# Window attention in eight chunks: scores of four images at once, and gelu as one image and then three

## The chip, the cores and the metric

One core of a Trainium2 chip. The metric is the device time of one launch in microseconds (us). Engines are named as in the profile: PE (TensorE) with PEld, its weight loads; DVE (VectorE); ACT (ScalarE); POOL (GpSimd); SP (SyncE).

## The reference

The kernel computes one block of a windowed transformer on x of shape 4 x 32 x 64 x 64 (images, channels, height, width), all in fp32. A window is 8 x 8 pixels, so 64 tokens of 32 channels; there are 4 heads of 8 channels. In short:

```python
xw = windows_of(x)                                  # (-1, 64, 32)
h = _ln(xw, ln1_g, ln1_b)
q, k, v = split(h @ qkv_w.T + qkv_b)                # 4 heads
attn = softmax(einsum('whnd,whmd->whnm', q * hd ** (-0.5), k) + bias)
o = einsum('whnm,whmd->whnd', attn, v)
xw = xw + (o @ proj_w.T + proj_b)
h = _ln(xw, ln2_g, ln2_b)
h = gelu(h @ fc1_w.T + fc1_b)                       # 32 -> 128
xw = xw + (h @ fc2_w.T + fc2_b)                     # 128 -> 32
```

## The kernel before

The four images lie on the 128 partitions, 32 channels each. The work is cut into NCH = 8 chunks; a chunk is one row of 8 windows in each image, 512 tokens. One chunk's attention has 8 units: a unit is four windows of one image, a tile of 128 x 512 scores.

PSUM has eight banks of 128 x 512. Before, S_PS is banks 0 and 1 (scores), T_PS banks 2 and 3 (transposed scores), FA and FB banks 4 and 5 (front: centering, variance, k, q, v), O_PS and D_PS banks 6 and 7 (attention output, projection, second norm).

Every engine runs its own program in order, counting semaphores tie the programs together, and the order is written out by hand. All but the closing loop is one software pipeline over c. In iteration c the *front* works for chunk f = c + 1, the scores for c, and the *back* for p = c - 1. The path of a unit is:

- `score` (PE, L656): q against masked keys, K = 32 rows of one image at row group C * g, windows in the two column halves. One call makes two units (two images) in the two S_PS banks and waits until both were read (`biased`).
- `add_bias` (DVE, L472) reads the bank, adds the table and writes one of six buffers s_sb; `find_max` (DVE, L482) takes the row maxima; `subtract_max` (POOL, L207) subtracts them. POOL also does `mask_keys` (L198) and `norm2` (L214).
- `turn` (PE, L677) transposes two units into the two T_PS banks; `exp_round` (ACT, L250) takes the exponential of both in one instruction.
- `attend` (PE, L691) multiplies four units by v and sums them for the denominator; `inv_den` (ACT, L311) and `divide` (DVE, L499) finish the softmax. t = 0 and 1 are the halves of a chunk.

The front of a chunk is `center1` (L620), `square1` (ACT, L258), `variance1` (L623), `inv_std1` (ACT, L264: Ln, then Exp), `norm1` (DVE, L490), `make_k` (L637), `make_v` (L648), `make_q` (L645), and ACT's `copy_k` (L272: a plain copy, two masked), `copy_v` (L296) and `copy_q` (L289). The back is `project` (L719), `residual` (DVE, L510), `center2` (L725), `keep2` (DVE, L515), `square2` (ACT, L320), `variance2` (L732), `inv_std2` (ACT, L326), `norm2`. Products of 64 x 64 tiles come from two helpers, `straight` (L605) and `crossed` (L611), which fill different tiles of the array, so one call of each stands side by side: variance2 with center1, make_k with project, make_q with center2. These three are called pairs. The PE order of an iteration is at L785 to L834: four scores, r = 0 to 3, with other work between each.

`up` (PE, L735) makes the hidden layer of a chunk, one image to a bank: banks 0 to 3 for chunk 0 and the odd ones (`low`), banks 3 to 6 for the rest, so bank 3 is shared. `gelu` (ACT, L334) takes two images to an instruction, those with the shared bank first; `down` (PE, L755) and `add_y` (DVE, L560) finish, and SP stores. up(0), gelu(0) and down(0) run in the last iterations; the closing loop (L836 to L841) does chunks 1 to 7. `up(c)` waits for the first gelu of chunk c - 1 alone (L744).

## Time and profile before

| What | us |
|---|---|
| Runs shown | 188.22, 189.28, 192.5 (median 189.28) |
| Profiled execution, its time | 188.29 |
| Profiled execution, its span | 186.6 |
| PE busy | 169.2 (91%) |
| ACT busy | 129.2 (69%) |
| DVE busy | 120.2 (64%) |
| PEld busy | 92.4 (50%) |
| POOL busy | 91.4 (49%) |

Busy is the union of an engine's instructions. Several matmuls can run at a time in different tiles of the array, so PE's busy time is less than the sum of its records. An fp32 matmul of the program gives two records.

### The profile page before, as it was taken

Reading aid. Unit: us, or ns where it says so; the run is one execution under the profiler, and the core shown is the slowest. Engines: PE = TensorE matmul, PEld = TensorE weight load, DVE = VectorE, ACT = ScalarE, POOL = GpSimd, SP = SyncE. Lnnn points to the kernel's source line nnn. Section 1 sums busy time; section 2 is a strip of 40 time slices with the busy share of each in tenths; the row PEclk is TensorE's granted clock in tenths of the full one; section 3 lists DMA queues with packets and bytes.
Section 4 is the critical chain, followed back from the end, with each engine's and each line's share of the span. In section 5 each row is a group of like instructions: output and inputs, shape, how many; then the busy total and the mean of one; then the engine's idle time right before and its main releaser. Section 6 shows DMA issues by size and latency. Waiting matters only on the chain.

```text
span 186.6 us, 6349 instructions
## 1 busy us (share of the span) xinstructions
PE 169.2 (91%) x2688; PEld 92.4 (50%) x2688; DVE 120.2 (64%) x220; ACT 129.2 (69%) x180; POOL 91.4 (49%) x103
## 2 busy tenths in 40 slices
PE   7976999999999999999999999999999878738882
PEld 7642465566456546565565565455655533102210
DVE  3486965978687677869786977677697821403222
ACT  4546595569677866868696779677843385798881
POOL 7402674647492856567484937584766540020000
PEclk9999999999999999999999999999999999999999
DMA  2840000000000000000000000000000000001323
GB/s 71 231 174 4 0 2 4 4 4 2 4 4 0 4 4 2 4 5 0 4 4 4 0 4 5 0 4 0 4 5 4 0 4 0 29 27 56 116 112 112
DMA packets 3245, 4.71 MB, mean 25 GB/s; under 512 B 946, under 2 KB 1298, under 8 KB 3218
## 3 DMA queue, kind: packets, MB, share of 16 engines
q1 hardware_dynamic: 2840, 4.23, 6.7%
q8 instruction: 21, 0.34, 0.8%
q0 software_dynamic: 256, 0.07, 0.4%
q14 instruction: 6, 0.05, 0.1%
q10 hardware_dynamic: 122, 0.01, 0.0%
HBM read 2.21 MB, written 2.10 MB: 23 GB/s over the span
## 4 chain that ended last, share of the span: by engine, by line
PE 67%; DVE 10%; ACT 10%; issue 5%; DMA 3%; POOL 3%; ACTq 1%; DVEq 0%; POOLq 0%
PE ps L670 17%; PE ps L686 12%; PE ps L605 9%; PE ps L704 9%; PE ps L711 7%; DVE s_sb L477 7%; ACT hid L342 5%; PE ps L651 4%; PE ps L751 4%; PE ps L629 3%; DMA raw_b<-in_L_conv_rpb_dram 3%; POOL raw_b L193 2%; DVE mx L487 1%; ACT rstd L330 1%; ACT pt L255 1%
## 5 line engine op out<-in xcount | busy, mean ns | idle before, releaser
L211 POOL TENSOR_TENSOR s_sb<-s_sb,mx 128x512 f32<-128x512 f32 x64 | 66.6, 1045 | 61.1 <-DVE mx L487 61.1
L477 DVE TENSOR_TENSOR s_sb<-ps,bias_t 128x512 f32<-128x512 f32 x64 | 43.9, 686 | 26.0 <-PE ps L670 25.0
L487 DVE TENSOR_REDUCE mx<-s_sb 128x8 f32<-128x512 f32 x64 | 43.9, 686 | 2.2
L670 PE MATMUL ps<-k_m,q_sb 32*64 32x256 f32 x512 | 35.0, 387 | 2.9 <-DVE s_sb L477 2.1
L686 PEld LDWEIGHTS ps<-ident,s_sb 128*128 128x128 f32 x256 | 27.5, 140 | 17.7 <-issue 10.3
L255 ACT ACTIVATE pt<-ps 128x1024 f32<-128x1024 f32 x32 | 32.5, 1016 | 5.1 <-PE ps L686 4.2
L686 PE MATMUL ps<-ident,s_sb 128*128 128x128 f32 x256 | 34.9, 279 | 0.0
L670 PEld LDWEIGHTS ps<-k_m,q_sb 32*64 32x64 f32 x512 | 16.4, 131 | 15.2 <-DVE s_sb L477 5.6
L704 PEld LDWEIGHTS ps<-pt,v_blk 128*32 128x32 f32 x1024 | 15.0, 110 | 8.1 <-ACT pt L255 6.0
L704 PE MATMUL ps<-pt,v_blk 128*32 128x64 f32 x1024 | 17.6, 220 | 1.5 <-ACT pt L255 1.5
L342 ACT ACTIVATE hid<-ps,fb 128x1024 f32<-128x1024 f32 x16 | 17.0, 1110 | 2.0 <-PE ps L751 2.0
L605 PE MATMUL ps<-h,wqk 64*64 64x512 f32 x64 | 17.0, 613 | 1.2 <-DVE h L494 1.2
L611 PE MATMUL ps<-x_sb,cent_m 64*64 64x512 f32 x64 | 17.2, 614 | 0.9 <-DVE x_sb L512 0.9
L562 DVE SCALAR_TENSOR_TENSOR y_sb<-ps,vec,x_sb 128x512 f32<-128x512 f32 (+1 forms) x9 | 6.2, 691 | 17.2 <-PE ps L765 17.2
L711 PE MATMUL ps<-pt,ones_h 128*32 128x256 f32 x256 | 16.7, 379 | 0.0
L217 POOL TENSOR_TENSOR h_sb<-h_sb,rstd 128x512 f32<-128x512 f32 x8 | 10.3, 1282 | 12.4 <-ACT rstd L332 12.4
L316 ACT ACTIVATE den<-ps 128x256 f32<-128x256 f32 x16 | 6.1, 384 | 11.0 <-PE ps L711 11.0
L506 DVE TENSOR_TENSOR att<-ps,den 128x256 f32<-128x256 f32 x16 | 6.7, 420 | 10.2 <-ACT den L318 10.2
L751 PE MATMUL ps<-h_sb,f_s 32*128 32x512 f32 x64 | 9.1, 637 | 4.5 <-ACT hid L342 4.5
L262 ACT ACTIVATE sq<-ps 128x512 f32<-128x512 f32 x8 | 4.8, 598 | 10.1 <-PE ps L611 10.1
L280 ACT ACTIVATE k_sb<-ps,bq 128x512 f32<-128x512 f32 x8 | 5.5, 688 | 9.0 <-PE ps L605 7.8
L651 PEld LDWEIGHTS ps<-wv,h 128*64 128x64 f32 x256 | 8.1, 138 | 6.5 <-issue 6.5
(92 smaller groups left out, 190.5 us busy)
## 6 DMA issues: line engine op xcount, KB each, us to landing
x_sb<-in_x_dram SPq DMA_DIRECT2D x8, 256.0 KB, 4.8
out_dram<-y_sb SPq DMA_DIRECT2D x7, 256.0 KB, 2.0
out_dram<-y_sb SPq DMA_DIRECT2D x2, 128.0 KB, 1.8
raw_b<-in_L_conv_rpb_dram POOLq DMA_DIRECT2D x8, 8.0 KB, 2.7
f_nat<-in_L_conv_fc_w_dram SPq DMA_DIRECT2D x2, 16.0 KB
w_nat<-in_L_conv_qkv_w_dram ACTq DMA_DIRECT2D x1, 12.0 KB
p_nat<-in_L_conv_proj_w_dram SPq DMA_DIRECT2D x1, 4.0 KB
vec_r<-in_L_conv_ln_g_dram ACTq DMA_DIRECT2D x1, 0.1 KB
```

The costliest lines, as they stand in the source:

```text
L211: pool.tensor_tensor(tile, tile, mx[:, n % 4, :].unsqueeze(2).to_broadcast([128, 2 * NH, NT]), ALU.subtract).then_inc(shifted, 1)
L255: act.activation(pt[:, n % 8:n % 8 + 2, :, :, :].rearrange("p u a k n -> p (u a k n)"), ps[:, 2:4, :].rearrange("p u n -> p (u n)"), ACT.E ...
L342: act.activation(hid[:, c % 2, 2 * pair:2 * pair + 2, :].rearrange("p g n -> p (g n)"), ps[:, b:b + 2, :].rearrange("p g n -> p (g n)"), A ...
L477: dve.tensor_tensor(s_sb[:, n % NSB, :, :, :].rearrange("p a h m -> p a (h m)"), S_PS[u].rearrange("p (a k) -> p a k", a=2), bias_t[:, :, ...
L487: dve.reduce_max(mx[:, n % 4, :], s_sb[:, n % NSB, :, :, :].rearrange("p a h m -> p (a h) m"), AX.X)\
L605: ins = pe.matmul(out[r:r + 64, :], w[r:r + 64, r:r + 64], rhs[r:r + 64, :], start=True, stop=True, tile_position=(r, r))
L611: ins = pe.matmul(out[64 - r:128 - r, :], w[r:r + 64, r:r + 64], rhs[r:r + 64, :], start=True, stop=True, tile_position=(r, 64 - r))
L670: ins = pe.matmul(S_PS[u][NT * ab:NT * (ab + 1), 256 * pr:256 * (pr + 1)], q_sb[C * g:C * (g + 1), c % 2, NT * w:NT * (w + 1)], k_m[C * g: ...
L686: ins = pe.transpose(T_PS[u][:, 128 * i:128 * (i + 1)], s_sb[:, n % NSB, pr, 2 * hp:2 * hp + 2, :].rearrange("p h m -> p (h m)"), ident[:, :])
L704: ins = pe.matmul(OD_PS[t][C * g:C * (g + 1), NT * wl:NT * (wl + 1)], v_blk[:, c % 2, G * (4 * t + wl) + g, 32 * (1 - hp):32 * (2 - hp)], ...
L711: ins = pe.matmul(OD_PS[t][C * g:C * (g + 1), 256:512], ones_h[:, hp, :], pt[:, (4 * t + g) % 8, :, hp, :], start=(hp == 0), stop=(hp == 1 ...
L751: ins = pe.matmul(ps[:, first_bank(c) + g, :], f1_s[C * g:C * (g + 1), :], h2_sb[C * g:C * (g + 1), c, :], start=True, stop=True, tile_pos ...
```

## The change

A score now makes four units, all four images, in four banks: `score(c, t)`, t = 0, 1. There are 2 calls of 32 records to a chunk, where there were 4 of 16; the transposes, exponentials, DVE and POOL instructions stay as many. The banks are dealt anew: 0 to 3 scores, bank 0 also variance1, make_v and make_q, bank 1 also attend(c, 0); 4 and 5 transposed scores; 6 (X_PS) center1 and make_k; 7 (Y_PS) attend(p, 1), project, center2, variance2.

The order of PE in iteration c becomes: score(c, 0), pair variance2(p-1)/center1(f), turn(p, 3), variance1(f), attend(p, 1), turn(c, 0), score(c, 1), turn(c, 1), pair make_k(f)/project(p), make_v(f), attend(c, 0), pair make_q(f)/center2(p), turn(c, 2). The other engines follow it: inv_den and divide of the first half move from the next iteration to this one, the Exp of inv_std2 moves behind an exponential, copy_v comes straight behind copy_k, copy_q behind inv_den. make_q now waits for copy_v, which reads its bank, and so does the very first score. up(0) moves ahead of attend(7, 1). In `gelu` the first instruction takes the one image in the shared bank, the second the three others. Not shown below: the same names in add_bias, find_max, subtract_max, the copies and the set-up, where only bank or index names change.

```diff
-        S_PS = [ps[:, 0, :], ps[:, 1, :]]
-        T_PS = [ps[:, 2, :], ps[:, 3, :]]
-        FA, FB = ps[:, 4, :], ps[:, 5, :]
-        O_PS, D_PS = ps[:, 6, :], ps[:, 7, :]
-        OD_PS = [O_PS, D_PS]
+        S_PS = [ps[:, g, :] for g in range(G)]
+        T_PS = [ps[:, 4, :], ps[:, 5, :]]
+        X_PS, Y_PS = ps[:, 6, :], ps[:, 7, :]
+        OD_PS = [S_PS[1], Y_PS]
...
             for c in range(-1, NCH + 2):
                 f = c + 1
-                for r in range(3):
-                    if there(c):
-                        subtract_max(c, r, 0)
-                        subtract_max(c, r, 1)
-                    if r == 0 and there(c - 2):
-                        norm2(c - 2)
+                if there(c):
+                    for g in range(G):
+                        subtract_max(c, 0, g)
+                if there(c - 2):
+                    norm2(c - 2)
+                if there(c):
+                    subtract_max(c, 1, 0)
                 if f >= 1 and there(f):
                     mask_keys(f)
                 if there(c):
-                    subtract_max(c, 3, 0)
-                    subtract_max(c, 3, 1)
+                    for g in range(1, G):
+                        subtract_max(c, 1, g)
...
+            def log_var2(p):
                 act.wait_ge(var2_ready, p + 1)
                 if p >= 1:
                     act.wait_ge(h2_ready, p)
-                act.activation(rstd2[:, :], FB, ACT.Ln, bias=eps[:, :]).then_inc(log2, 1)
+                act.activation(rstd2[:, :], Y_PS, ACT.Ln, bias=eps[:, :]).then_inc(log2, 1)
+
+            def inv_std2(p):
                 act.wait_ge(log2, p + 1)
                 act.activation(rstd2[:, :], rstd2[:, :], ACT.Exp, scale=-0.5).then_inc(rstd2_ready, 1)
...
-                for pair in ((1, 0) if low(c) else (0, 1)):
-                    b = first_bank(c) + 2 * pair
-                    act.activation(hid[:, c % 2, 2 * pair:2 * pair + 2, :].rearrange("p g n -> p (g n)"),
-                                   ps[:, b:b + 2, :].rearrange("p g n -> p (g n)"),
+                shared = 3 - first_bank(c)
+                for images in (slice(shared, shared + 1), slice(0, 3) if low(c) else slice(1, 4)):
+                    banks = slice(first_bank(c) + images.start, first_bank(c) + images.stop)
+                    act.activation(hid[:, c % 2, images, :].rearrange("p g n -> p (g n)"),
+                                   ps[:, banks, :].rearrange("p g n -> p (g n)"),
                                    ACT.Gelu, bias=fb1[:, :]).then_inc(gelu_ready, 1)
 
             for c in range(-1, NCH + 2):
                 f, p = c + 1, c - 1
-                if there(p):
-                    inv_den(p, 0)
                 if there(f):
                     square1(f)
                 if c == 0:
                     blank_values(1)
                 if there(p - 1):
+                    log_var2(p - 1)
+                if there(p):
+                    exp_round(p, 3)
+                if there(f):
+                    inv_std1(f)
+                if there(p - 1):
                     inv_std2(p - 1)
                 if there(p):
-                    exp_round(p, 3)
-                if there(f):
-                    inv_std1(f)
-                if there(p):
                     inv_den(p, 1)
-                if there(c):
-                    exp_round(c, 0)
-                if there(f):
-                    copy_k(f)
-                    if f == 0:
-                        copy_q(f)
-                    if f == 0:
-                        copy_v(f)
-                if there(c):
-                    exp_round(c, 1)
-                if f >= 1 and there(f):
-                    copy_v(f)
-                if f >= 1 and there(f):
-                    copy_q(f)
                 if p == NCH - 1:
                     act.preload_act_table_set("gelu_and_others")
                     gelu(0)
                     act.preload_act_table_set("natural_log_exp_and_others")
+                if there(c):
+                    exp_round(c, 0)
+                    exp_round(c, 1)
+                if there(f):
+                    copy_k(f)
+                    if f == 0:
+                        copy_q(f)
+                    copy_v(f)
+                if there(c):
+                    inv_den(c, 0)
+                if f >= 1 and there(f):
+                    copy_q(f)
                 if there(p):
                     square2(p)
...
             for c in range(-1, NCH + 1):
                 f, p = c + 1, c - 1
                 if there(c):
-                    add_bias(c, 0, 0)
-                    find_max(c, 0, 0)
-                    add_bias(c, 0, 1)
-                    find_max(c, 0, 1)
-                if there(p):
-                    divide(p, 0)
-                if there(c):
-                    add_bias(c, 1, 0)
-                    find_max(c, 1, 0)
-                    add_bias(c, 1, 1)
-                    find_max(c, 1, 1)
+                    for g in range(G):
+                        add_bias(c, 0, g)
+                        find_max(c, 0, g)
                 if there(f):
                     norm1(f)
                 if there(p):
                     divide(p, 1)
                 if there(c):
-                    add_bias(c, 2, 0)
-                    find_max(c, 2, 0)
+                    for g in range(2):
+                        add_bias(c, 1, g)
+                        find_max(c, 1, g)
                 if there(p):
                     residual(p)
                 if there(c):
-                    add_bias(c, 2, 1)
-                    find_max(c, 2, 1)
-                    add_bias(c, 3, 0)
-                    find_max(c, 3, 0)
+                    for g in range(2, G):
+                        add_bias(c, 1, g)
+                        find_max(c, 1, g)
+                    divide(c, 0)
                 if there(p):
                     keep2(p)
-                if there(c):
-                    add_bias(c, 3, 1)
-                    find_max(c, 3, 1)
...
             def wait_center1(f):
                 pe.wait_ge(x_in[f], 16)
                 if f >= 1:
-                    pe.wait_ge(v_copied, f)
+                    pe.wait_ge(k_copied, f)
+                if f >= 2:
+                    pe.wait_ge(k_scaled, f - 1)
...
             def variance1(f):
                 pe.wait_ge(squared1, f + 1)
-                if f >= 3:
-                    pe.wait_ge(log2, f - 2)
                 if f >= 1:
-                    pe.wait_ge(q_copied, f)
-                pe.matmul(FB, mean_m[:, :], sq1[:, :], start=True, stop=True).then_inc(var1_ready, 1)
+                    pe.wait_ge(biased, unit_of(f - 1, 0, 0) + 1)
+                pe.matmul(S_PS[0], mean_m[:, :], sq1[:, :], start=True, stop=True).then_inc(var1_ready, 1)
 
...
             def wait_q(f):
-                pe.wait_ge(k_copied, f + 1)
                 if f >= 1:
-                    pe.wait_ge(k_scaled, f)
+                    pe.wait_ge(v_copied, f + 1)
...
             def make_v(f):
+                if f >= 1:
+                    pe.wait_ge(biased, unit_of(f - 1, 1, 0) + 1)
+                else:
+                    pe.wait_ge(log1, 1)
                 for w in range(NW):
                     for hh in range(2):
-                        ins = pe.matmul(FA[NT * hh:NT * (hh + 1), NT * w:NT * (w + 1)], h1[:, f % 2, w, :],
+                        ins = pe.matmul(S_PS[0][NT * hh:NT * (hh + 1), NT * w:NT * (w + 1)], h1[:, f % 2, w, :],
                                         wv[:, hh, :, :].rearrange("p k d -> p (k d)"), start=True, stop=True,
                                         tile_position=(0, NT * hh))
...
-            def score(c, r):
-                if r == 0:
+            def score(c, t):
+                if t == 0:
                     pe.wait_ge(q_copied, c + 1)
                     pe.wait_ge(k_masked, c + 1)
                     if c >= 1:
                         pe.wait_ge(k_scaled, c)
-                n = unit(c, r, 0)
-                if n >= 2:
+                        pe.wait_ge(divided, 2 * (c - 1) + 1)
+                    else:
+                        pe.wait_ge(v_copied, 1)
+                elif there(c + 1):
+                    pe.wait_ge(log1, c + 2)
+                n = unit_of(c, t, 0)
+                if n:
                     pe.wait_ge(biased, n)
                 for pr in range(2):
                     for ab in range(2):
-                        w = 4 * (r // 2) + 2 * pr + ab
-                        for u in range(2):
-                            g = 2 * (r % 2) + u
-                            ins = pe.matmul(S_PS[u][NT * ab:NT * (ab + 1), 256 * pr:256 * (pr + 1)],
+                        w = 4 * t + 2 * pr + ab
+                        for g in range(G):
+                            ins = pe.matmul(S_PS[g][NT * ab:NT * (ab + 1), 256 * pr:256 * (pr + 1)],
                                             q_sb[C * g:C * (g + 1), c % 2, NT * w:NT * (w + 1)],
                                             k_m[C * g:C * (g + 1), c % 2, :, NT * w:NT * (w + 1)],
                                             start=True, stop=True, tile_position=(C * g, NT * ab))
...
                 pe.wait_ge(v_copied, c + 1)
-                if c == 0:
+                if t == 0:
+                    pe.wait_ge(biased, unit_of(c, 1, 1) + 1)
+                elif c == 0:
                     pe.wait_ge(late_ready, 1)
-                elif t == 0:
-                    pe.wait_ge(x1_ready, c)
                 else:
-                    pe.wait_ge(kept2, c)
+                    pe.wait_ge(log2, c)
                 for wl in range(4):
...
             def up(c):
                 pe.wait_ge(h2_ready, c + 1)
                 if c == 0:
                     pe.wait_ge(late_ready, 1)
                     pe.wait_ge(biased, NU)
-                    pe.wait_ge(expd, NU)
+                    pe.wait_ge(divided, 2 * NCH - 1)
                 elif c == 1:
                     pe.wait_ge(gelu_ready, 2)
                 else:
                     pe.wait_ge(gelu_ready, 2 * c - 1)
                 if c == 2:
                     pe.wait_ge(y_ready, 1)
-                    pe.wait_ge(q_copied, NCH)
-                    pe.wait_ge(log2, NCH)
-                    pe.wait_ge(x1_ready, NCH)
+                    pe.wait_ge(k_copied, NCH)
+                    pe.wait_ge(k_scaled, NCH - 1)
...
@@ -795,17 +796,16 @@
                     center1(f)
                 if there(p):
                     turn(p, 3)
-                if there(c):
-                    score(c, 1)
                 if there(f):
                     variance1(f)
-                if there(p):
-                    attend(p, 1)
                 if p == NCH - 1:
                     up(0)
+                if there(p):
+                    attend(p, 1)
                 if there(c):
                     turn(c, 0)
-                    score(c, 2)
+                    score(c, 1)
+                    turn(c, 1)
                 if there(f):
                     wait_k(f)
                 if there(p):
@@ -817,8 +817,7 @@
                 if there(f):
                     make_v(f)
                 if there(c):
-                    turn(c, 1)
-                    score(c, 3)
+                    attend(c, 0)
                 if there(f):
                     wait_q(f)
                 if there(p):
@@ -831,7 +830,6 @@
                     down(0, 4, slice(0, TC))
                 if there(c):
                     turn(c, 2)
-                    attend(c, 0)
```

## Rows read from the trace of the kernel before

**Rows 1.** Stages; columns: us, busy us (instructions) of each engine, clock, DMA share
```profile
14.38:30.23 15.85, 14.27 (x214) 7.95 (x214) 11.26 (x18) 10.79 (x14) 9.64 (x10) 1.00 0.01 3
...
30.23:134.10 103.87, 103.42 (x1884) 60.13 (x1880) 79.55 (x126) 77.01 (x118) 63.19 (x66) 1.00 0.01 3
...
165.81:186.60 20.79, 13.89 (x112) 3.41 (x112) 5.42 (x8) 14.83 (x14) 0.09 (x1) 0.98 0.24 89
```

**Rows 2.** The same for one period of the inner loop
```profile
82.16:99.48 17.32, 17.25 (x319) 10.03 (x315) 13.25 (x21) 13.02 (x20) 10.83 (x12) 1.00 0.01 2
```

**Rows 3.** Timeline of TensorE in that period: start, us, engine, line, tiles, idle before
```profile
83.19 0.65 PE L605 MATMUL ps<-sq,mean_m 64*64 64x512 f32 x2
...
84.20 1.09 PE L686 MATMUL ps<-ident,s_sb 128*128 128x128 f32 x8
...
86.39 1.13 PE L629 MATMUL ps<-sq,mean_m 128*128 128x512 f32 x2
...
87.45 0.94 PEld L704 LDWEIGHTS ps<-pt,v_blk 128*32 128x32 f32 x64 [0.76 <-ACT pt L255]
87.45 1.10 PE L704 MATMUL ps<-pt,v_blk 128*32 128x64 f32 x64
...
89.34 1.10 PE L686 MATMUL ps<-ident,s_sb 128*128 128x128 f32 x8
...
90.37 1.09 PE L670 MATMUL ps<-k_m,q_sb 32*64 32x256 f32 x16
...
91.39 0.65 PE L605 MATMUL ps<-h,wqk 64*64 64x512 f32 x2
...
92.41 1.15 PE L651 MATMUL ps<-wv,h 128*64 128x64 f32 x32
...
93.49 1.09 PE L686 MATMUL ps<-ident,s_sb 128*128 128x128 f32 x8
```

**Rows 4.** Closing loop: one cycle of the timeline, and gelu's group of the page
```profile
178.05 2.12 ACT L342 ACTIVATE hid<-ps,fb 128x1024 f32<-128x1024 f32 x2 [0.34 <-PE ps L751]
...
179.30 1.14 PE L751 MATMUL ps<-h_sb,f_s 32*128 32x512 f32 x8 [0.32 <-ACT hid L342]
...
180.38 1.06 PE L765 MATMUL ps<-hid,f_st 128*32 128x512 f32 x8
180.50 2.12 ACT L342 ACTIVATE hid<-ps,fb 128x1024 f32<-128x1024 f32 x2 [0.34 <-PE ps L751]
...
L342 ACT ACTIVATE hid<-ps,fb 128x1024 f32<-128x1024 f32 x16 | 17.0, 1110 | 2.0 <-PE ps L751 2.0
```

**Rows 5.** Timeline of DVE and POOL in the period of rows 2
```profile
83.31 0.69 DVE L477 TENSOR_TENSOR s_sb<-ps,bias_t 128x512 f32<-128x512 f32 x1 [1.63 <-PE ps L670]
...
84.03 0.69 DVE L487 TENSOR_REDUCE mx<-s_sb 128x8 f32<-128x512 f32 x1
...
84.63 0.68 DVE L477 TENSOR_TENSOR s_sb<-ps,bias_t 128x512 f32<-128x512 f32 x1
...
84.80 1.04 POOL L211 TENSOR_TENSOR s_sb<-s_sb,mx 128x512 f32<-128x512 f32 x1 [2.00 <-DVE mx L487]
```

**Rows 6.** Timeline of ACT in the period of rows 2
```profile
84.37 0.60 ACT L262 ACTIVATE sq<-ps 128x512 f32<-128x512 f32 x1 [1.24 <-PE ps L611]
...
84.86 0.68 ACT L330 ACTIVATE rstd<-ps,eps 128x512 f32<-128x512 f32 x1
...
86.11 1.01 ACT L255 ACTIVATE pt<-ps 128x1024 f32<-128x1024 f32 x1
...
92.52 0.69 ACT L280 ACTIVATE k_sb<-ps,bq 128x512 f32<-128x512 f32 x1 [0.97 <-PE ps L605]
...
93.10 1.44 ACT L285 ACTIVATE k_m<-ps,bkm,hmask 128x512 f32<-128x512 f32 x2
```

**Rows 7.** Timeline of ACT before the first score
```profile
13.51 1.20 ACT L308 ACTIVATE v_blk<-ps 64x512 f32<-64x512 f32 x2 [0.39 <-PE ps L651]
```

**Rows 8.** Timeline of TensorE: the last turn of the last chunk
```profile
151.30 1.09 PE L686 MATMUL ps<-ident,s_sb 128*128 128x128 f32 x8
```

More of the change, by code:

```diff
@@ L255, in exp_round @@
                 act.activation(pt[:, n % 8:n % 8 + 2, :, :, :].rearrange("p u a k n -> p (u a k n)"),
-                               ps[:, 2:4, :].rearrange("p u n -> p (u n)"), ACT.Exp).then_inc(expd, 2)
+                               ps[:, 4:6, :].rearrange("p u n -> p (u n)"), ACT.Exp).then_inc(expd, 2)
             def square1(f):
@@ L261, in square1 @@
                     act.wait_ge(var1_ready, f)
-                act.activation(sq1[:, :], FA, ACT.Square).then_inc(squared1, 1)
+                act.activation(sq1[:, :], X_PS, ACT.Square).then_inc(squared1, 1)
             def inv_std1(f):
```

90 lines of the change are left out of this document (45 added, 45 removed).

## The prediction, made before the changed kernel was run

> **What bounds the kernel now.** I read the busy time by stage first, then one inner period, then the order of time inside it, engine by engine, and last the closing loop. By stages [rows 1], six periods of 17.31 us (30.23 to 134.10) hold 103.87 of the 186.6 us; the reader is to see that TensorE is busy 103.42 of them and that DVE (79.55), ACT (77.01) and POOL (63.19) are not near it. In one period [rows 2] it is 17.25 of 17.32 us against 13.25, 13.02 and 10.83. So the period is the sum of TensorE's pieces, and only an edit that takes TensorE time away, or that opens a gap, can move it. The starts of its pieces [rows 3] give each one's price: score 1.03 (82.16, the start in rows 2, to 83.19), a pair of 64-row products 1.01 and 1.02, variance1 1.06, attend with its sums 1.89, turn 1.03, make_v 1.08. Four scores, three pairs, four turns, two attends, one variance1, one make_v: 4.12 + 3.05 + 4.12 + 3.78 + 1.06 + 1.08 = 17.2. The closing loop [rows 1, 4] is another matter: TensorE is busy 13.89 of 20.79 us there, and gelu's first half, up, and the next gelu follow one another every 2.45 us (178.05 to 180.50).
>
> **Score of four images.** Two scores of 16 matmul records per window half become one of 32. Today's form fills two of four row groups and both column halves. variance1 sends two records of 512 columns, 1024 in all, through the whole array in 1.06 [rows 3]; today's score sends 1024 through each of four tiles (16 records of 256) in the same time. Up sends 1024 through each of four row groups into four banks in 1.14 [rows 4]: row groups run side by side. Attend sends 1024 through each of four column groups, in 64 records, in 1.10 [rows 3]: so do column groups, and twice the issues of the new score don't hold it up. The new score again has 1024 columns for each tile, in eight tiles. So I take 1.05 us for the new score, the old 1.03 and a little for twice the issues. Bounds: 1.03, as if the second half were free, and 2.06, as if it were two old ones in a row. The trace shows each factor, not the two together (four row groups with two halves), so both ends stay in the range; 1.05 is nearest to both rows. TensorE's sum is then 17.2 - 2.05 = 15.2 us.
>
> **Which waits the new order opens.** I walk one inner period, 0 being the start of score(c,0), with the starts of rows 3, DVE and POOL by rows 5 and ACT by rows 6. TensorE: score 0, pair variance2/center1 1.05, turn(p,3) 2.07, variance1 3.10, free at 4.16. The old order had score(c,1) between that turn and that attend; now the exponential of turn(p,3) has variance1 alone as cover. ACT squares 1.17 us after the pair starts (84.37 against 83.19), its Ln of var2 follows 0.49 later, and the exponential 0.6 after that: 3.32 to 4.33. Attend starts at 4.39: **gap 0.23**. Then turn(c,0) 6.29 and score(c,1) 7.32. Here DVE must have evacuated four banks: with a pair of add and max every 1.32 us (83.31 to 84.63) from 1.16 on, the fourth add ends at 5.80, so 1.5 us of room. POOL needs 1.04 a tile and follows DVE: the four tiles are ready at 3.7, 5.0, 6.3, 7.6. turn(c,1) must not overwrite the two turn banks before exp(c,0) has read them: turn(c,0) ends near 7.4, the exponential takes 1.01, so 8.54 against TensorE free at 8.37: **gap 0.17**. Pair make_k/project 9.57 (norm1 ended at 7.1, divide(p,1) at 7.8), make_v 10.59, attend(c,0) 11.67, free at 13.57. make_q now shares bank 0 with make_v and waits for copy_v, which stands behind copy_k: k's copy starts 1.13 after its pair (92.52 against 91.39), at 10.70, its two masked copies at 11.28, copy_v at 12.6 to 13.8. Pair make_q/center2 at 13.85: **gap 0.28**. Then turn(c,2) 14.87, next score(c+1,0) at 15.90. For that score, the last add ended near 13.8, divide(c,0) near 15.1, copy_q at 15.7; POOL with eight tiles, norm2 and mask_keys is through at 15.9, and turn(p,3) wants its last tile at 17.9. Behind the waiting make_q are turn(c,2) and the next score; behind late attends only TensorE's own order. New period 15.90 against 17.32, 1.42 saved; six of them: **8.5 us**. Bounds of the gaps: none (period 15.2) and 17.5, if each hand-over costs the 0.76 us that attend's weights wait for ACT today [rows 3]. I keep 0.68 in all, from the walk.
>
> **First and last chunk.** In chunk 0 nothing of an earlier chunk fills TensorE, so DVE and POOL set it: tiles ready at 5.0 and 7.65; score(0,1) at 5.85; turn(0,1) to 8.25; make_k, make_v, attend to 12.2; copy_v 12.5, make_q 12.55, turn 13.55, next score at 14.6, against 15.85 today [rows 1]: **1.25 saved**. The first score now waits for copy_v, which ends at 13.51 + 1.20 [rows 7], instead of 14.38: **0.4 lost**. In the last chunk there is no f work to fill; the four pairs of DVE after score(7,1) (8.4 to 13.7), divide, keep2 to 15.4, square2, and variance2 put turn(7,3) at 17.2. Today it is 151.30 - 134.10 = 17.2 [rows 8]: the halved scores are worth nothing there. Behind it the rsqrt's Exp moves behind the last exponential: **0.2 saved**, as that exponential starts 0.2 earlier.
>
> **Gelu of one image, then three.** up(c+1) waits for gelu's first instruction alone. 512 elements take 0.60 and 1024 take 1.01 [rows 6], 0.41 for 512; a gelu of 1024 is 1.11 [rows 4], so the first is now 0.69 and the second 1.53, starting 0.1 before the first ends; both together stay at 2.12. The chain gelu, up, gelu falls from 2.45 to 2.03. But another takes its place: a chunk's up start, 1.20 to its gelu (rows 4: 179.30 to 180.50), 2.12 for both gelus, 0.05 to down, about 1.02 to the next up but one, 4.39 for two chunks, 2.2 each. Walked from 165.81, the seventh gelu starts 13.2 us on, today 14.7: **1.5 saved**. Bounds: nothing, and 2.1 (six times 0.35, where ACT never rests at 2.1).
>
> **The sum.** -0.4 + 1.25 + 8.5 + 0.2 + 1.5 = 11.05. The profiled execution took 188.29 us for a span of 186.6; it becomes 177.2, with a span of 175.5. The median of the runs shown is 189.28, 1.0 higher, so my 177.2 stands nearer to the low runs.
>
> **A rule that speaks against it.** Rows 5 show the evacuation of one score bank and its maximum at 1.32 us, so four at once take 5.3, while the score that fills them takes 1.05. The Trainium skill (page TensorEngine Tiling (Array Packing), section Performance Considerations, PSUM Bottleneck) says that tiling speeds TensorE but not the emptying of PSUM, which may become the bottleneck after a fourfold speed-up. By the sum above DVE has 15.90 - 13.25 = 2.6 us left in a period; by the rule the hand-over is late, and that is the first rival.
>
> **Rivals.**
> First, DVE becomes the bound. All four banks are handed back at once, so DVE stands still through each score. For: it waits 1.63 us once already [rows 5]. Against: behind the last add of a round stand a max, norm1 and divide, or a max, divide and keep2, 1.8 us. If these come too late to fill, the period is 13.25 + 2 x 1.2 of score + 1.0 for divide and keep2 late behind ACT and center2 = 16.6; six times 0.7 saved is 4.3 in place of 8.5, total 6.85: 181.4 us.
> Second, the exponentials gate TensorE. For: today it already waits 0.76 on one, at L704 [rows 3], and two of the four lose a score as cover. Against: ACT is busy 13.02 of 17.32. With 0.45 more at each of three hand-overs the period is back at 17.3 and what is left is 2.5: 185.7 us.
> Third, slower than before: eight tiles don't run together. The new score then takes 2.06. The place is TensorE alone: 15.2 + 2.0 + 0.5 of gaps (that before turn(c,1) is covered) = 17.7, 0.4 more than now, which makes 2.3 in six; chunk 0 +0.3, last chunk +1.0, start +0.4, tail -0.2, gelu -1.5: 2.3 slower, 190.6 us. It decides from a score of about 1.8 us (16 x 0.77 eats the 11 us and what the gaps absorb). Against: rows 3 and 4, above.
> Fourth, the gelu split does nothing, since down keeps up away: 178.7 us, inside the likeliest case's range.
>
> **How the numbers follow.** Forecast 0.71, with a range of its own from 174.5 (half of the gaps gone, 2.0, and gelu at its better bound, 0.6) to 180 (each gap twice as wide gives 4.1 more, most of it); first rival 0.15; second 0.09; third 0.05. A measurement of this kernel can tell about 2% from no change, which is 185.5 and 193.1 against the median. Faster takes the forecast and the first rival, 0.86; the second and most of the third are within 2%, 0.11; slower 0.03, for a score well over two old ones. The range of 174.5 to 183.5 takes in the forecast and the first rival.
>
> **What would show it.** Right: the new score's 32 records in 1.05 to 1.15 us; starts of score(c,0) 15.9 us apart; TensorE idle before attend(p, 1), before turn(c, 1) and before make_q by some 0.2 each, released by ACT; DVE waiting for PE twice a period for about a microsecond; gelus of 128x512 near 0.69 and 128x1536 near 1.53, 2.2 us a chunk. Wrong: scores near 2 us; TensorE waiting for DVE before score(c,1); waits on ACT of over 0.6 in each period; a period of over 16.6.

## The result, and the profile after

The changed kernel took 178.85 us (median of four runs, 177.82 to 179.19) against 189.70 for the kernel before beside it: a ratio of 0.9443, 95% interval 0.9366 to 0.952. Faster, by 5.6%; 177.2 was forecast, in a range of 174.5 to 183.5. The ratio is of fast runs alone and leaves out the 192.5 us run of the kernel before. The profiled execution is the fastest of the four, 177.82 us with a span of 176.1 at a mean granted clock of 1.00. The other three have spans of 176.9 to 177.4 at 0.987 to 0.99; part 6 of the experiments and the last section take that up.

The stages of the kernel after, from one score(c, 0) to another, and in the last line one inner period (columns as in [rows 1]):

```profile
0.00:15.29 15.29, 12.48 (x86) 8.67 (x87) 8.38 (x44) 7.67 (x9) 5.78 (x17) 1.00 0.49 145
15.29:30.01 14.72, 12.89 (x214) 7.09 (x214) 11.48 (x18) 10.21 (x14) 9.58 (x10) 1.00 0.01 3
30.01:125.48 95.47, 91.10 (x1881) 55.04 (x1880) 78.99 (x126) 74.97 (x118) 63.69 (x65) 1.00 0.01 3
125.48:156.89 31.41, 23.68 (x397) 11.54 (x396) 15.09 (x24) 19.81 (x26) 12.02 (x11) 1.00 0.03 10
156.89:176.10 19.21, 13.75 (x112) 3.27 (x112) 5.42 (x8) 14.61 (x14) 0.09 (x1) 1.00 0.26 96
77.72:93.64 15.92, 15.16 (x315) 9.13 (x314) 13.17 (x21) 12.73 (x21) 10.82 (x11) 1.00 0.01 2
```

Against [rows 1]: the six periods went from 103.87 to 95.47 us, 8.40 less, and TensorE's busy time in them from 103.42 to 91.10, 12.3 less. A period against [rows 2] lost 2.09 us of TensorE's work (17.25 to 15.16) and 1.40 of length. The difference is what TensorE now stands idle, 0.76 of 15.92 us against 0.07. DVE, ACT and POOL have nearly the work that they had: 13.17, 12.73 and 10.82 us in the period, against 13.25, 13.02 and 10.83.

The timeline of TensorE in that period (start, us, idle before in brackets), one record or more of each piece:

```profile
77.72 1.12 PE L673 MATMUL ps<-k_m,q_sb 32*64 32x256 f32 x32
78.77 0.65 PE L601 MATMUL ps<-sq,mean_m 64*64 64x512 f32 x2
...
79.79 1.09 PE L689 MATMUL ps<-ident,s_sb 128*128 128x128 f32 x8
80.72 1.02 PE L625 MATMUL ps<-sq,mean_m 128*128 128x512 f32 x2
82.09 1.10 PE L707 MATMUL ps<-pt,v_blk 128*32 128x64 f32 x64 [0.35 <-ACT pt L260]
...
83.99 1.09 PE L689 MATMUL ps<-ident,s_sb 128*128 128x128 f32 x8
85.01 1.12 PE L673 MATMUL ps<-k_m,q_sb 32*64 32x256 f32 x32
86.33 1.06 PE L689 MATMUL ps<-ident,s_sb 128*128 128x128 f32 x8 [0.20 <-ACT pt L260]
87.33 0.65 PE L601 MATMUL ps<-h,wqk 64*64 64x512 f32 x2
...
88.35 1.15 PE L650 MATMUL ps<-wv,h 128*64 128x64 f32 x32
89.43 1.10 PE L707 MATMUL ps<-pt,v_blk 128*32 128x64 f32 x64
...
91.60 0.65 PE L601 MATMUL ps<-h,wqk 64*64 64x512 f32 x2 [0.20 <-ACT v_blk L313]
...
92.62 1.09 PE L689 MATMUL ps<-ident,s_sb 128*128 128x128 f32 x8
```

From score to next piece is 78.77 - 77.72 = 1.05 us for 32 records, where 16 took 1.03. Idle time stands in front of three pieces only: attend(p, 1) and turn(c, 1), each behind an exponential (L260), and make_q's pair, behind v's copy (L313).

DVE in the same period, the two waits and the last add of each round of four:

```profile
78.90 0.69 DVE L483 TENSOR_TENSOR s_sb<-ps,bias_t 128x512 f32<-128x512 f32 x1 [1.30 <-PE ps L673]
...
82.87 0.68 DVE L483 TENSOR_TENSOR s_sb<-ps,bias_t 128x512 f32<-128x512 f32 x1
...
86.19 0.69 DVE L483 TENSOR_TENSOR s_sb<-ps,bias_t 128x512 f32<-128x512 f32 x1 [0.70 <-PE ps L673]
...
90.81 0.68 DVE L483 TENSOR_TENSOR s_sb<-ps,bias_t 128x512 f32<-128x512 f32 x1
```

The banks are free at 83.55, and TensorE wants them at 85.01: DVE waits for the score, the score never for DVE. In the first chunk the second score does wait for DVE, 0.23 us:

```profile
21.32 1.12 PE L673 MATMUL ps<-k_m,q_sb 32*64 32x256 f32 x32 [0.23 <-DVE s_sb L483]
```

In the closing loop the two gelus by shape, and a cycle of TensorE:

```profile
L350 ACT ACTIVATE hid<-ps,fb 128x1536 f32<-128x1536 f32 x7 | 10.7, 1535 | 0.0
L350 ACT ACTIVATE hid<-ps,fb 128x512 f32<-128x512 f32 x7 | 4.8, 687 | 0.6 <-PE ps L752 0.6
```

```profile
163.44 1.07 PE L766 MATMUL ps<-hid,f_st 128*32 128x512 f32 x8 [0.17 <-ACT hid L350]
164.44 1.14 PE L752 MATMUL ps<-h_sb,f_s 32*128 32x512 f32 x8
165.51 1.07 PE L766 MATMUL ps<-hid,f_st 128*32 128x512 f32 x8
```

From the first gelu of this loop (156.89) to the seventh (170.02) are 13.13 us, where the kernel before took 180.50 - 165.81 = 14.69 [rows 1, 4]. ACT's idle time in front of gelus is 0.6 us over seven chunks; before it was 2.0 in the page's row for all of them [rows 4].

### The profile page after: what moved, and what is told of

The parts are those of the page before. It is cut to its first block, busy times and chain, and to the rows that moved or that the text cites. A ratio compares the mean times of both kernels' runs of the same rounds, so it can differ in the third digit from the quotient of the medians.

```text
span 176.1 us, 6350 instructions
## 1 busy us (share of the span) xinstructions
PE 153.9 (87%) x2688; PEld 85.6 (49%) x2688; DVE 119.4 (68%) x220; ACT 127.3 (72%) x180; POOL 91.2 (52%) x103
## 3 DMA queue, kind: packets, MB, share of 16 engines
q1 hardware_dynamic: 2840, 4.23, 7.0%
## 4 chain that ended last, share of the span: by engine, by line
PE 56%; ACT 29%; issue 7%; DVE 6%; ACTq 1%; DVEq 0%
PE ps L689 17%; PE ps L601 13%; ACT pt L260 9%; PE ps L673 6%; ACT k_m L290 5%; ACT hid L350 5%; PE ps L707 5%; ACT v_blk L313 5%; PE ps L714 4%; DVE s_sb L483 3%; PE ps L583 2%; PE ps L766 2%; PE ps L752 2%; PE ps L607 2%; DVE mx L493 1%
## 5 line engine op out<-in xcount | busy, mean ns | idle before, releaser
L260 ACT ACTIVATE pt<-ps 128x1024 f32<-128x1024 f32 x32 | 32.6, 1020 | 13.9 <-PE ps L689 13.8
L707 PEld LDWEIGHTS ps<-pt,v_blk 128*32 128x32 f32 x1024 | 15.0, 110 | 10.9 <-ACT pt L260 10.4
L673 PE MATMUL ps<-k_m,q_sb 32*64 32x256 f32 x512 | 17.9, 387 | 1.0 <-ACT v_blk L313 0.8
L607 PE MATMUL ps<-x_sb,cent_m 64*64 64x512 f32 x64 | 17.5, 625 | 0.9 <-DVE x_sb L518 0.9
L350 ACT ACTIVATE hid<-ps,fb 128x512 f32<-128x512 f32 (+1 forms) x16 | 16.7, 1111 | 0.7 <-PE ps L752 0.6
L673 PEld LDWEIGHTS ps<-k_m,q_sb 32*64 32x64 f32 x512 | 9.6, 131 | 4.7 <-issue 2.4
L207 POOL TENSOR_SCALAR k_m<-k_sb,hmask 128x512 f32<-128x512 f32 x14 | 9.5, 692 | 3.7 <-ACT k_sb L285 3.7
```

What stands on the lines that cost most here:

```text
L260: act.activation(pt[:, n % 8:n % 8 + 2, :, :, :].rearrange("p u a k n -> p (u a k n)"), ps[:, 4:6, :].rearrange("p u n -> p (u n)"), ACT.E ...
L350: act.activation(hid[:, c % 2, images, :].rearrange("p g n -> p (g n)"), ps[:, banks, :].rearrange("p g n -> p (g n)"), ACT.Gelu, bias=fb1 ...
L607: ins = pe.matmul(out[64 - r:128 - r, :], w[r:r + 64, r:r + 64], rhs[r:r + 64, :], start=True, stop=True, tile_position=(r, 64 - r))
L673: ins = pe.matmul(S_PS[g][NT * ab:NT * (ab + 1), 256 * pr:256 * (pr + 1)], q_sb[C * g:C * (g + 1), c % 2, NT * w:NT * (w + 1)], k_m[C * g: ...
L707: ins = pe.matmul(OD_PS[t][C * g:C * (g + 1), NT * wl:NT * (wl + 1)], v_blk[:, c % 2, G * (4 * t + wl) + g, 32 * (1 - hp):32 * (2 - hp)], ...
```

## Experiments

My theory: TensorE is the bound of a period, eight tiles of the score work side by side, and what is given back is three short waits on ACT. The rivals: the gain comes from elsewhere (the gelus, the order), or DVE's emptying of the banks is the bound. Ratios are to the kernel before, run beside each version, with their 95% intervals.

**1. The two parts apart.** The gelu part alone, put into the kernel before:

```
-for pair in ((1, 0) if low(c) else (0, 1)):
-    b = first_bank(c) + 2 * pair
+shared = 3 - first_bank(c)
+for images in (slice(shared, shared + 1), slice(0, 3) if low(c) else slice(1, 4)):
+    banks = slice(first_bank(c) + images.start, first_bank(c) + images.stop)
```

> The kernel before with the new gelu alone (one image, then three). My theory: the closing loop goes from 2.45 us a chunk to 2.2, bound by the chain of two chunks up, both gelus, down, up; 1.5 us off the whole, nothing else moves: about 186.8 in the profiled execution (ratio to before 0.992). If what the changed kernel won in the closing loop came from the new order of banks or from an earlier start, this kernel stays at 188.3.

Measured: 188.23 us (186.63 to 188.79), ratio 0.9893 (0.9792 to 0.9993). The median is 1.65 us below that of the kernel before beside it (189.88), about the 1.5 expected, though the interval reaches to within 0.1% of no change. The profiled execution, at 188.39 us, is no faster than the profiled one before (188.29), against the 186.8 expected. Its trace shows why: windows of 4 us at the head of the closing loop (granted clock is the number behind POOL's), and TensorE's timeline there.

```profile
164.00:168.00 4.00, 1.57 (x13) 0.54 (x8) 0.00 (x0) 3.94 (x5) 1.26 (x1) 0.86 0.00 1
168.00:172.00 4.00, 4.00 (x28) 0.67 (x24) 0.75 (x1) 2.61 (x4) 0.00 (x0) 0.71 0.00 0
```

```profile
167.01 2.09 PE L752 MATMUL ps<-h_sb,f_s 32*128 32x512 f32 x8 [2.42 <-ACT hid L343]
169.03 1.68 PE L766 MATMUL ps<-hid,f_st 128*32 128x512 f32 x8
170.63 1.14 PE L752 MATMUL ps<-h_sb,f_s 32*128 32x512 f32 x8
```

TensorE stood still for 2.42 us, and then up took 2.09 where it takes 1.14 [rows 4]: part of the stretch was granted the 1.2 GHz level (the granted clock is 0.50 over the 2 us from 168.0). Behind it the loop runs at 4.37 us for two chunks (gelus at 171.84, 176.22 and 180.59), the 2.2 us a chunk of the walk. From the first gelu of the loop (166.22) to the seventh are 14.37 us, 0.32 less than before and 1.24 more than in the changed kernel, where the clock kept 1.00. The first score also came 0.43 later than before, at 14.81. Together that is the 0.1 us by which this span, 186.7, is over the one before.

The other way round, the changed kernel with gelu in pairs again (the same diff backwards):

> The changed kernel with the old gelu in pairs. If the two parts add up: closing loop back at 2.45 a chunk, 1.5 us more than the changed kernel (about 179.3 in the profiled execution), the inner period unchanged at 15.9. If the parts lean on each other the two differences of this and of the kernel before with the new gelu would not be equal.

Measured: 180.38 (180.24 to 180.39), ratio 0.9498 (0.9429 to 0.9567), 1.5 above the changed kernel; a period is 15.92 here too. So the gelu part is worth about 1.5 us of the 10.9, and all the rest is the score and its order. The profile has such a dip of the clock too, 0.72 and 0.85 in two windows of 4 us from 157.0 on.

**2. Is it the eight tiles?** First only the order of issue, images 0 and 1 through all windows, then 2 and 3:

```
+for half in range(2):
     for pr in range(2):
         for ab in range(2):
...
-            for g in range(G):
+            for g in range(2 * half, 2 * half + 2):
```

> The changed kernel, but each score issues images 0 and 1 for all its windows first and then images 2 and 3: the same 32 records, banks, waits and order of everything else. My theory (the gain is that eight tiles run side by side): TensorE issues in order, so the second half starts only when the first half's last records start, 0.7 after it began: a score of 1.75 to 2.05 us, a period of 16.4 to 16.7 (0.7 to 1.0 twice, less the 0.2 that stood before turn(c,1)), and 8 to 12 us of the gain of 10.5 gone: 186 to 190. Rival (the gain is the new order, with fewer hand-overs between PE and DVE, not the array): the score is longer but the time stays near 178 to 180.

Measured: 179.19 (178.24 to 180.39), ratio 0.9441 (0.936 to 0.9522): no different from the changed kernel. My expectation was wrong: it said a period of 16.4 to 16.7, and it is 15.96 (77.54 to 93.50). TensorE's timeline:

```profile
77.54 1.15 PE L674 MATMUL ps<-k_m,q_sb 32*64 32x256 f32 x32
78.62 0.65 PE L601 MATMUL ps<-sq,mean_m 64*64 64x512 f32 x2
```

1.08 us to the next piece: the second half ran beside the first although all of it was issued behind it. This order of issue doesn't serialise the halves; so I let TensorE wait on the semaphore of its own first half:

```
 for half in range(2):
+    if half:
+        pe.wait_ge(scored, n + 2)
```

> The changed kernel with images 0 and 1 first, and images 2 and 3 only when TensorE's own records of the first two are complete: the two halves can't share the array. (Issuing them in this order without the wait cost 1.07 us a score in place of 1.05, against my 1.75 to 2.05: the array took both side by side all the same.) My theory: 1.03 + 1.05 + 0.1 to 0.2 of wait, 2.2 us a score, 1.15 more, twice a period, less the 0.24 that stood before turn(c,1): period 17.9 to 18.0, 13 to 15 us more than the changed kernel, slower than before. Rival (the gain is the new order): the time stays near 179, a period of at most 16.3.

Measured: 193.96 (193.57 to 194.09), ratio 1.0182 (1.0135 to 1.023): 1.8% above the kernel before, an interval clear of no change, though not clear of 2%. The score, the piece behind it, and a period:

```profile
84.78 2.30 PE L676 MATMUL ps<-k_m,q_sb 32*64 32x256 f32 x32
87.01 0.65 PE L601 MATMUL ps<-sq,mean_m 64*64 64x512 f32 x2
```

```profile
84.78:102.83 18.05, 17.26 (x316) 10.01 (x315) 13.34 (x21) 12.75 (x21) 10.84 (x11) 1.00 0.01 2
```

With 2.23 us for the score (87.01 - 84.78) the new order is 15.1 us longer in all, and its period is 0.7 over the old one's 17.32. Some of that is the price of the wait itself, as two of the old scores take 2 x 1.03 = 2.06. An estimate without it, 0.17 less twice a period, is 18.05 - 0.34 = 17.71, still above 17.32. So the whole gain of the inner loop is the two halves side by side. Without that the new order is a loss: the third rival had mechanism and sign right, and its condition does not hold.

**3. Does DVE stand close to the bound?** Maxima that nobody reads, into a tile of their own, behind one tile of four, and behind three.

```
+if g == 1:      # or: if g < 3
...
+    dve.reduce_max(mx_x[:, len(extra) % 4, :],
+                   s_sb[:, n % NSB, :, :, :].rearrange("p a h m -> p (a h) m"), AX.X)\
```

> The changed kernel with one more row maximum of 0.69 us on DVE, into a tile that nobody reads, for one of four units: 16 more, two in a period, 1.2 to 1.4 us. My theory: DVE has 2.6 us left in a period and the walk has room where they stand, so the six inner periods stay within 0.1 of 15.92; only the last chunk, which hangs on DVE, and the first gain up to 0.7 each: 0.7 to 1.4 us in all. Rival (DVE's emptying of four banks at once is already the bound): 16 x 0.6 = 9.6 us more.

Measured: 179.53 (179.12 to 180.41), ratio 0.9462 (0.9386 to 0.9537). The period:

```profile
77.87:93.79 15.92, 15.16 (x315) 9.13 (x315) 14.16 (x24) 12.72 (x20) 10.86 (x12) 1.00 0.01 3
```

DVE has 1 us more to do and the period is 15.92 as before: it has that much free. All six periods together take 95.47 us (30.16 to 125.63), the same as in the changed kernel. The first chunk takes 0.60 more and the last, up to the first gelu, 0.59 more (125.63 to 157.63 is 32.00, against 31.41). The medians are only 0.68 apart; the four runs of each kernel spread over 1.3 to 1.4 us. The first chunk, where DVE has 1.18 us more to do:

```profile
14.84:30.16 15.32, 12.90 (x215) 7.10 (x215) 12.66 (x20) 10.21 (x14) 9.59 (x10) 1.00 0.01 3
```

Of its two extra maxima the first shows in full: score(0, 1) stands 6.62 us behind score(0, 0) here (21.46 - 14.84), and 6.03 in the changed kernel. The second costs nothing: from there to the next score are 8.70 and 8.69.

> The changed kernel with one more row maximum of 0.69 us on DVE for three of four units, 6 in a period: 3.6 to 4.1 us, over the 2.6 that DVE has left. My theory: here DVE becomes the bound, with 13.25 + 3.6 and what it waits for scores: a period of 17.2 to 17.8, 8 to 12 us more than the changed kernel; TensorE then waits for DVE before score(c,1). If one more a half had cost nothing because DVE's records overstate it, this would cost little too: under 3 us.

Measured: 195.91 (195.78 to 196.57, three runs), ratio 1.0292 (1.024 to 1.0343). A fourth execution, the profiled one, had a granted clock of 0.56 over its whole span and took 256.21; it is left out (with it the median is 196.24). So the profile is from one more execution:

> The kernel with three more row maxima a half again, for its profile (its time was 196.2, 17.4 us more than the changed kernel, over my 8 to 12). If DVE is the bound, DVE is busy near 95% of the inner periods, a period is close to 18.1 us, and the start of score(c,1) and score(c+1,0) hangs on DVE's adds and divide. If something else made it dearer than its 3.6 us of DVE a period allow, DVE has idle time of over 1.5 us a period.

It took 195.01 us, with these periods and scores:

```profile
85.82:103.36 17.54, 15.56 (x315) 9.35 (x315) 16.44 (x28) 12.72 (x20) 10.88 (x12) 1.00 0.01 3
```

```profile
93.55 1.12 PE L682 MATMUL ps<-k_m,q_sb 32*64 32x256 f32 x32 [0.29 <-DVE s_sb L485]
...
103.36 1.12 PE L682 MATMUL ps<-k_m,q_sb 32*64 32x256 f32 x32 [1.08 <-DVE att L521]
```

This is the first rival's world: DVE busy 94% of a period, and both scores released by DVE. It takes 3.3 us of extra DVE work (16.44 - 13.17) to get there, of which 1.6 show. The period is within the 17.2 to 17.8 expected at first, and below the 18.1 expected for this execution; the total is above the 8 to 12 us more, because the first chunk and the last took 3.15 and 4.23 us more than in the changed kernel:

```profile
15.33:33.20 17.87, 14.37 (x216) 8.25 (x217) 14.94 (x24) 10.21 (x14) 9.41 (x10) 0.90 0.01 2
...
138.43:174.07 35.64, 26.82 (x396) 12.46 (x396) 18.91 (x31) 19.90 (x26) 12.55 (x12) 0.90 0.03 9
```

DVE has 3.5 and 3.8 us more in them, but the granted clock is also 0.90 in both. In the first chunk the two can be told apart in part: up to score(0, 1) the clock is whole and the way is 1.77 us longer (7.80 against 6.03), which is DVE's; behind it the clock is 0.83 and the way 1.37 longer. How much of that and of the last chunk's 4.23 is DVE's and how much the clock's stays open.

**4. The waits on ACT.** The mask copies of k that ACT makes (L290) go to POOL, so that v's copy comes earlier. POOL subtracts one more maximum ahead of them:

```
-    for h in range(2, NH):
+    for h in range(NH):
...
-        for h in range(2):
-            ins = act.activation(k_m[:, f % 2, h, :], X_PS, ACT.Identity, bias=bkm[:, h:h + 1],
```

> The changed kernel with the two masked copies of k on POOL (four masks there) in place of ACT, and POOL's second subtraction of the half ahead of them. The gap before make_q is copy_v behind copy_k's masked copies: it goes, 0.28 a period, so a period of 15.65 and 1.6 to 2.0 us off the whole. Rival: copy_q is as late as before (ACT has the same chain inv_den, copy_q to the next score) and the period stays at 15.9; or POOL, now at 12.2 of 15.7 us, brings the last subtractions late for turn(p,3) and the period grows.

Measured: 177.05 (176.7 to 177.58), ratio 0.9295 (0.9253 to 0.9337), 1.8 less than the changed kernel. The period, and make_q's pair, which has no idle time before it now:

```profile
76.91:92.56 15.65, 15.09 (x316) 9.14 (x315) 13.17 (x22) 11.53 (x18) 12.20 (x14) 1.00 0.01 2
```

```profile
90.51 0.65 PE L595 MATMUL ps<-h,wqk 64*64 64x512 f32 x2
```

The 0.27 us off a period is the gap that was predicted at 0.28. POOL took 1.4 us more work in a period for it and is at 12.20 of 15.65. On top of that, turn(c, 1) behind the pair make_k/project, so that the exponential has the pair as cover; on ACT, k's copy moves ahead of exp(c, 1):

```
-            turn(c, 1)
...
+            if there(c):
+                turn(c, 1)
```

> The same with the pair make_k/project ahead of turn(c,1), and copy_k ahead of exp(c,1) on ACT. The pair covers the exponential that turn(c,1) waits for (0.24 gone), but exp(c,1) ends at 11.6 in the walk and attend(c,0) could start at 11.5: 0.1 to 0.15 comes back there. Period 15.5 to 15.6, 2.2 to 3.2 us less than the changed kernel. Rival: an exponential is late by as much wherever it stands, and the period is that of the kernel with the masks on POOL alone.

Measured: 176.99 (176.25 to 177.61), ratio 0.9288 (0.9241 to 0.9335), a period of 15.55, as expected. That gap went, but attend(c, 0)'s weights now wait 0.22 us for exp(c, 1), and it starts 1.23 behind make_v instead of 1.08: 0.1 a period is left, which the totals don't tell apart from no change. Against the changed kernel it is 1.9 less, where 2.2 to 3.2 were expected.

**5. The start.** The first chunk's v goes through another bank, so the first score needn't wait for its copy:

```
-src = S_PS[0][r].rearrange("p (w k d) -> p w k d", k=2, d=HD)
+src = (S_PS[0] if f else T_PS[1])[r].rearrange("p (w k d) -> p w k d", k=2, d=HD)
...
-        pe.wait_ge(v_copied, 1)
```

> The changed kernel with the first chunk's make_v in a bank of the transposes (bank 5), so that the first score doesn't wait for copy_v. My theory: the first score starts when DVE has masked the first keys, 0.4 to 0.5 earlier for the same start of the kernel, chunk 0 passes it on, and the whole is 0.4 to 0.5 less than the changed kernel (178.3 to 178.5). Rival: chunk 0 hangs on DVE's table and masks or on ACT's blank tile of 1.9 us, and the time stays at 178.8.

Measured: 178.42 (178.06 to 178.84, six runs), ratio 0.9413 (0.9364 to 0.9463): 0.43 below, about what was expected, though the intervals of the two overlap. ACT's copy of v and TensorE's first score, in the changed kernel and here:

```profile
13.95 1.19 ACT L313 ACTIVATE v_blk<-ps 64x512 f32<-64x512 f32 x2 [0.39 <-PE ps L650]
...
15.29 1.12 PE L673 MATMUL ps<-k_m,q_sb 32*64 32x256 f32 x32 [0.76 <-ACT v_blk L313]
```

```profile
14.52 1.20 ACT L313 ACTIVATE v_blk<-ps 64x512 f32<-64x512 f32 x2 [0.39 <-PE ps L650]
...
15.18 1.12 PE L671 MATMUL ps<-k_m,q_sb 32*64 32x256 f32 x32
```

From the copy's start to the score are 1.34 us in the first, 0.66 in the second (0.87 in the kernel before, [rows 7, 1]). The wait is gone, but this execution got to the copy 0.57 us later.

**6. The clock at the head of the closing loop.** Nine products of zeros are issued where TensorE stands still ahead of it. They only occupy TensorE; nothing reads them.

```
+pe.wait_ge(expd, NU)
+for _ in range(9):
+    pe.matmul(T_PS[1][:, 0:128], blank[:, :], blank[:, :], start=True, stop=True)
```

> The changed kernel with nine matmuls of zeros into a free bank (bank 5) between up(1) and up(2), where TensorE otherwise stands still for 2.4 us ahead of the closing loop. In this kernel's other executions the mean granted clock was 0.987 to 0.99 and the span 0.8 to 1.3 us longer than in the profiled one with 1.0; in the profiles of four experiments the granted clock falls to half for some 2 to 3 us at the head of the closing loop, right behind that stand. Theory: with the matmuls TensorE doesn't stand still there, the clock stays at 1.0 in that stretch in every execution, and the median falls from 178.85 to 177.8 to 178.1 and agrees with the profiled 177.82. Rival: the fall comes from what TensorE did before 153 us (it stands still four times from 143 on), and nothing changes; or the nine matmuls delay up(2) and cost up to 0.5.

Measured: 177.60 (177.51 to 179.6, six runs), ratio 0.9406 (0.9337 to 0.9474). Four runs are at 177.51 to 177.6, with a clock of 0.998 or 0.999, two at 179.4 and 179.6, with 0.99. The profile of one of the four:

```profile
152.50:156.50 4.00, 3.91 (x28) 2.34 (x29) 0.07 (x1) 2.76 (x5) 1.26 (x1) 1.00 0.20 70
156.50:160.50 4.00, 3.54 (x28) 1.06 (x27) 0.75 (x1) 4.00 (x4) 0.00 (x0) 1.00 0.00 0
```

TensorE is kept busy through the stretch and the clock stays whole behind it. The two runs at 0.99 have no profile, and where their clock fell stays open. It may be at the place, some 7 us ahead of the loop, where it fell in three other profiles (see the last section); the products stand behind it and can't cover it. The intervals of this kernel and the changed one overlap, but the clocks of all runs speak for the products: with them (here and in part 7) 10 of 12 runs have 0.997 or more, and of the 39 runs of the changed kernel and its variants without them 2 have.

**7. All together**: the masks on POOL, turn(c, 1) behind the pair, the first v apart and the products of zeros.

> All together: masks on POOL, the pair ahead of turn(c,1), the first make_v apart, the matmuls of zeros before the closing loop. If the parts add up: period 15.55 as with the first two, 0.45 off the start, closing loop at full clock: 175.3 to 176.2, and at least 1 us less than the 176.99 of the first two alone. If the clock's part fails, 176.5.

Measured: 174.95 (174.24 to 175.37, six runs), ratio 0.9225 (0.9176 to 0.9275): 3.9 us less than the changed kernel, the fastest version here, and better than expected. The clock is 0.997 to 1.0 in all six runs.

## Why the prediction was right

**The sum.** 11.05 us were predicted for the profiled execution, and the spans differ by 186.6 - 176.1 = 10.5. By its terms, predicted and measured:

| term | predicted | measured |
|---|---|---|
| start to the first score | -0.4 | -0.91 (14.38 to 15.29) |
| chunk 0 | +1.25 | +1.13 (15.85 to 14.72) |
| six periods | +8.5 | +8.40 |
| last chunk, to the first gelu | +0.2 | +0.3 (31.71 to 31.41) |
| first to seventh gelu | +1.5 | +1.56 |
| the rest | 0 | 0.0 |
| in all | +11.05 | +10.5 |

**The score.** 1.05 predicted, 1.05 measured. The factors that the trace before showed one by one (row groups side by side in up, column groups in attend) do hold together. The wait inserted between the halves shows that this is what pays in the inner loop: 2.23 for the score puts the total above the kernel before.

**The walk.** From 77.72 on, turn(p, 3) was predicted at 2.07 and came at 2.07, attend(p, 1) at 4.39 and 4.37, score(c, 1) at 7.32 and 7.29, turn(c, 1) at 8.54 and 8.61, make_q's pair at 13.85 and 13.88, the next score at 15.90 and 15.92. The three gaps are where they were put, by the releasers that were named: 0.35, 0.20 and 0.20 in the timeline's brackets, where 0.23, 0.17 and 0.28 were forecast. The first is wider because variance1 starts 0.1 earlier than in the walk (3.00 instead of 3.10), while the exponential behind it comes when it was said to; the period doesn't feel it. DVE's fourth add was to end at 5.80 and ends at 83.55 - 77.72 = 5.83. The durations that the walk was built from are the same after the change: an add 0.68, a maximum 0.69, an exponential 1.02.

**The other rivals.** The exponentials do gate TensorE, as the second rival had it, but by 0.55 us a period (0.35 and 0.20), where the walk had 0.40, and not by 0.45 more at each hand-over. The period stays at 15.92 and not at 17.3. The fourth, that the gelu split does nothing, is ruled out by the closing loop (13.13 against 14.69) and by the kernel with gelus in pairs, 1.5 us slower.

**The rival of the rule.** DVE empties four banks in 5.3 us and keeps a score waiting nowhere in a period. One more maximum leaves the period at 15.92, and three more make it 17.54. The Trainium skill (page TensorEngine Tiling (Array Packing), section Performance Considerations, PSUM Bottleneck) says that after a fourfold speed-up of TensorE the copying out of PSUM may become the bottleneck. The trace agrees in part for the first chunk, where score(0, 1) waits 0.23 for DVE and one of two extra maxima shows in full, and not for the six periods.

**The last chunk.** turn(7, 3) was put 17.2 us behind score(7, 0) and comes 142.56 - 125.48 = 17.08 behind it, 17.2 in the kernel before [rows 8]: the halved scores are worth 0.1 us there. One more maximum in each half makes that chunk 0.59 longer (part 3), so DVE is on its path.

**The term that was off** is the start: 0.91 lost instead of 0.4. The wait for copy_v explains 1.34 - 0.87 = 0.47 of it, as predicted. The other 0.44 is that the whole chain comes later, v's copy at 13.95 instead of 13.51 [rows 7]: the first products of centring (L607) start 0.11 later and take 1.41 instead of 1.08. That isn't the change, since three profiles with the changed kernel's code up to there (gelu in pairs, one more maximum, the products of zeros) have the copy at 13.43 to 13.56. Over the profiles of all kernels, the one at a clock of 0.56 left out, it starts anywhere from 13.36 to 14.52, and the four records of centring take from 1.07 to 1.97 us. Why they differ stays open: the profile's granted clock is 1.00 there in each.

**The median** lies 1.0 us above the profiled execution, and the prediction gave a number nearer to the low runs, which it was. Six profiles of kernels without the products of zeros (the two of part 1, the order of issue, one more maximum, the two of part 4) have the granted clock down at the head of the closing loop, and the two with the products in neither place. Three (the waiting score, the first v apart, and the second execution of three more maxima) have it down some 7 us ahead of the loop, at center2 of the last chunk and the down behind it; the last of them also at two places further ahead. The changed kernel's own profile and that of the kernel before have no such fall before TensorE is done. That the three other runs of the changed kernel owe their 0.987 to 0.99 to the same place is likely, but none of them has a profile.

## What to carry to other kernels

Price a new tile form from its factors: if rows show row groups side by side in one operation and column groups in another, with equal columns for each tile, the product may come at the same price, as it did here; keep the dearer end in the range until it is measured. Then walk the new order by hand over every engine, instruction by instruction, and count the waits that it opens: here the walk gave 0.68 us back of the 2.05 that it saved, and one of the three could be had again by moving two copies to an engine with room. Spend extra work on a bound's neighbour (a maximum that nobody reads) to learn how far off it is, stage by stage, since the first and the last chunk may hang on another engine than the rest.

## What the runs showed of the hardware that I had not expected

Products in different row groups overlap over a whole half of the score: sixteen issued behind sixteen others finish within 1.08 us together, as when they alternate (1.05). With a wait on a semaphore between them the halves stand apart, and then they take 2.23.

The granted clock falls to the 1.2 GHz level for about 3 us at the head of the closing loop in six profiles, after TensorE has stood still for 2.42 to 2.85 us. In the gelu-alone kernel up takes 2.09 there instead of 1.14, and the first down 1.68 instead of 1.07. Shorter stands can be enough: in three profiles it falls at center2 of the last chunk, behind stands of 1.48 and 0.85 us with the project products between them, as here with the first v apart (1.51 instead of 1.08; the granted clock is 0.66 in 150 to 152 and 0.50 in 152 to 154).

```profile
150.13 1.51 PE L607 MATMUL ps<-x_sb,cent_m 64*64 64x512 f32 x4 [0.85 <-DVE x_sb L518]
```

It does not fall each time: the profiled execution of the changed kernel stands still as long at the head of the loop and keeps 1.00, and so does that of the kernel before, with 2.85.

```profile
157.68 1.14 PE L752 MATMUL ps<-h_sb,f_s 32*128 32x512 f32 x8 [2.42 <-POOL h_sb L221]
```

No run here shows why the same stretch dips in one execution and not in the next.
